# An expert's 176 inner rows as 112 and 64 in place of 88 and 88, and the 64 rows' two halves stacked in one operand

## The chip, the core and the metric

One Trainium2 chip, one of its cores. The engines are named as the profile names them: PE is TensorE (PEld its weight loads), DVE is VectorE, ACT is ScalarE, POOL is GpSimd, SP is the queue that starts most transfers. The metric is the device time of one execution, in microseconds (us).

## The reference

A transformer layer with adaptive layer norm, then a mixture of experts. The change touches the second part only: 2048 tokens of width 256, 16 experts of which each token takes 4, with an inner width of 176, and one shared expert with an inner width of 704.

```
g = jnp.einsum('nh,ehi->eni', h, w_gate)            # i = 176
u = jnp.einsum('nh,ehi->eni', h, w_up)
y = jnp.einsum('eni,eih->enh', jax.nn.silu(g) * u, w_down)
routed = jnp.einsum('enh,ne->nh', y, comb)          # comb: 4 experts a token
shared = jax.nn.silu(h @ sh_gate) * (h @ sh_up) @ sh_down   # 704 wide
return routed + sg * shared
```

## The kernel before

**How numbers are held.** Each matmul operand is kept as a high half (the value rounded to the matmul's format) and a low half (the rest). A product is three matmuls, in `PARTS`: high by high, high by low, low by high, given as (stationary, moving) pairs (0,0), (0,1), (1,0). ACT writes the high half with a copy out of PSUM, DVE the low half with a subtraction (`low_half`, L954, which also serves all other operands).

**The blocks.** Attention and the dense feed-forward take the first 665 us or so. Then the tokens are sorted by expert into 79 blocks of 128 rows. The weights of all experts lie in one tile, `wE`, and a block reads its expert's at an offset that PE loads into a register (`value_load`, L1864). For block i:

- PE turns the block's input (`turn_block`, L1855, two transposes); ACT (`high_hT`, L841) and DVE (`low_hT`) write its halves.
- PE computes gate and up together (`block_gate_up`, L1870): six matmuls of 352 columns. ACT takes silu (L847), DVE multiplies (L1372) into `hid_b`, 128 tokens by 176.
- PE turns `hid_b` (`turn_hidden`, L1881) as two transposes of 88 columns, into partitions 0 to 87 of one bank, beside each other. ACT (`high_hidT`, L853) and DVE (`low_hidT`) write the halves, one 88x256 instruction each.
- PE multiplies by the down weights (`block_down`, L1893): for each of the two groups of 88 rows the three `PARTS`, six matmuls of 256 columns that add up in one bank. ACT scales the result into `y_ring` (L861) and POOL scatters it (L628).

PE's order is written out by hand: in turn i it issues `turn_block(i+2)`, `block_gate_up(i+1)`, `turn_hidden(i)`, `block_down(i-1)`. So a block's down matmuls come one turn after its own transposes. All small tiles have two buffers.

**The shared expert.** 704 rows are five chunks of 128 and one of 64 (`SC_LAST`). For each of the four groups of 512 tokens and each chunk, `shared_gate_up` makes the hidden values and `shared_down` (L1831) multiplies by the down weights: 4 sub-blocks of 128 tokens by three matmuls of 256 columns, twelve a chunk, on 64 partitions for the last chunk. Two groups run before the blocks (calls 0 to 11), two after them (12 to 23). Call 11 stands just before the first `turn_block` of the loop.

Of the kernel before, what the change touches and what calls it, by code (L numbers as in the profile page):

```python
# [25 lines left out]
SC_FULL = I_SH // P  # L26
SC = SC_FULL + 1
SC_LAST = I_SH - SC_FULL * P
# [6 lines left out]
FRONT = FRONT_G * SC  # L35


HALF = I_MOE // 2
GU = 2 * I_MOE
EW = KD * GU + 2 * D  # L40

# [28 lines left out]
def adaln_moe_kernel(nc, x, condT, ada_w, bias, bqk, bv, wqkv, wo, w1, w2, router, shw_in, we_in, table, ident, out):  # L70
# [4 lines left out]
    ACT = mybir.ActivationFunctionType  # L75
# [20 lines left out]
    with ExitStack() as ctx:  # L96
# [20 lines left out]
        wE_flat = at("wE", 0, E * 2 * EW, f32r)  # L117
# [51 lines left out]
        id_sb = sb("id_sb", [P, P])  # L169
# [80 lines left out]
        h_blk, sil_b, hid_b = (blocks_own(m, n) for m, n in ((RING, HROW), (2, I_MOE), (2, I_MOE)))  # L250
# [22 lines left out]
            return (shw_b if late else shw)[:, first:first + w]  # L273

        def sh_down(late, c, s):
            rows = P if c < SC_FULL else SC_LAST
            first = 2 * SW * c + (s + 1) * sh_cols(c) - D
            return (shw_b if late else shw)[0:rows, first:first + D]

# [154 lines left out]
        def gated(i, rows):  # L434


            r = pair_of(i)
            return UP[r][:, :] if rows == P else GATE[r][0:rows, :]
# [4 lines left out]
        def pair_of(i):  # L443

            return (i + (i >= FRONT)) % 2
# [211 lines left out]
        def _(act):  # L657
# [191 lines left out]
            def high_hidT(i):  # L849
                act.wait_ge(s_hid_turned, i + 1)  # L850
                if i >= 2:
                    act.wait_ge(s_down_b, i - 1)
                nc.scalar.activation(hidT_b[0:HALF, i % 2, 0], HIDT_B[i % 2][0:HALF, 0:2 * P], ACT.Copy)\  # L853
                    .then_inc(s_hidT_high, 1)

            def keep_y(i):
# [57 lines left out]
        def _(dve):  # L914
# [38 lines left out]
            def low_half(target, whole, high):  # L953
                return nc.vector.tensor_tensor(target, whole, high.bitcast(f32), ALU.subtract)  # L954
# [355 lines left out]
            def shared_low(i):  # L1310
                rows = P if i % SC < SC_FULL else SC_LAST
                dve.wait_ge(s_hidden_high, i + 1)
                r = pair_of(i)
                hid = sh_hid[i >= FRONT]
                low_half(hid[0:rows, r, 1], gated(i, rows), hid[0:rows, r, 0]).then_inc(s_hidden_low, 1)

            def keep_shared(g):

# [54 lines left out]

            def low_hidT(i):
                dve.wait_ge(s_hidT_high, i + 1)
                low_half(hidT_b[0:HALF, i % 2, 1], HIDT_B[i % 2][0:HALF, 0:2 * P], hidT_b[0:HALF, i % 2, 0])\
                    .then_inc(s_hidT_low, 1)

            def destinations(n, own):

# [110 lines left out]
        def _(pe):  # L1491
# [327 lines left out]
            def shared_down(i):  # L1819
                g, c = divmod(i, SC)  # L1820
                rows = P if c < SC_FULL else SC_LAST
                pe.wait_ge(s_hidden_low, i + 1)
                if i == 0:
                    pe.wait_ge(s_h_kept, 2 * TG)
                elif i == FRONT:
                    pe.wait_ge(s_y_kept, BLOCKS)
                elif c == 0:
                    pe.wait_ge(s_sh_kept, BG * g)
                for b in range(BG):
                    for n, (s, m) in enumerate(PARTS):  # L1830
                        last = nc.tensor.matmul(DOWN[b // 2][:, D * (b % 2):D * (b % 2) + D],  # L1831
                                                sh_hid[i >= FRONT][0:rows, pair_of(i), s, T * b:T * b + T],
                                                sh_down(i >= FRONT, c, m),
                                                start=c == 0 and n == 0 and b % 2 == 0,
                                                stop=c == SC - 1 and n == len(PARTS) - 1, skip_group_check=True)
                last.then_inc(s_sh_down, 1)

            def blocks_to_all():
# [37 lines left out]
            def turn_hidden(i):  # L1876
                pe.wait_ge(s_hid, i + 1)
                if i >= 2:
                    pe.wait_ge(s_hidT_low, i - 1)
                for k in range(2):  # L1880
                    last = nc.tensor.transpose(HIDT_B[i % 2][0:HALF, P * k:P * k + P],  # L1881
                                               hid_b[i % 2][:, HALF * k:HALF * k + HALF], id_sb[:, :])
                last.then_inc(s_hid_turned, 1)

            def block_down(i, first):
                pe.wait_ge(s_hidT_low, i + 1)
                if i < 2:
                    pe.wait_ge(s_sh_kept, BG * FRONT_G)
                else:
                    pe.wait_ge(s_y_kept, i - 1)  # L1890
                for k in range(2):
                    for n, (s, m) in enumerate(PARTS):
                        last = nc.tensor.matmul(Y_B[i % 2][:, 0:D], hidT_b[0:HALF, i % 2, s, P * k:P * k + P],  # L1893
                                                wE_flat[0:HALF, bass.ds(first + (m * EW + KD * GU + D * k), D)],
                                                start=k == 0 and n == 0, stop=k == 1 and n == len(PARTS) - 1)
                last.then_inc(s_down_b, 1)

            for i in range(FRONT):
# [108 lines left out]
```

## Time and profile before

| | |
|---|---|
| median of 3 runs | 953.63 us (953.49 to 954.85) |
| profiled execution | 957.57 us, of which the span of the trace is 955.8 us |
| PE busy | 906.9 us (95%) |
| DVE, ACT, POOL busy | 571.2, 487.8, 271.9 us |
| block down matmuls (L1893) | 474, busy 75.7 us |
| shared down matmuls on 64 rows | 48 of 288 |

In the trace's rows a matmul (PE) is listed with the time from its start to its modelled end. Matmuls overlap, so the step from one start to the next is what one costs, not the length in its row. A weight load (PEld) belongs to each matmul and normally runs beside the matmul ahead of it. `88*128` in a row means 88 contraction rows by 128 stationary columns.

### The profile page before, as it was taken

To read this page: it belongs to the slowest core of one execution; us is meant where nothing else is said; L and a number is where in the kernel's file an instruction comes from. 1 tells how busy PE (TensorE), PEld (TensorE's weight loads), DVE (VectorE), ACT (ScalarE), POOL (GpSimd) and SP (SyncE) were. 2 spreads that over 40 slices of the span, in tenths; PEclk is the share of its full clock that TensorE was granted. 3 is DMA by queue.
4 is the path that set the end of the run, shared out by engine and by line. 5 is a ranking of instruction groups with operands and counts; after the bars stand their busy time and mean duration, and the time that the engine had idled before them with its cause. 6 is when DMAs were issued, how large, how long until landed. Compare 5 with 4: busy or idle time off the path is not lost.

```text
span 955.8 us, 17681 instructions
## 1 busy us (share of the span) xinstructions
PE 906.9 (95%) x5693; PEld 808.8 (85%) x5693; DVE 571.2 (60%) x1301; ACT 487.8 (51%) x1300; POOL 271.9 (28%) x220
## 2 busy tenths in 40 slices
PE   4899999999999999996999999999989899999996
PEld 4788989898989889895898877877878899999885
DVE  5844545545455464547547567775776655555786
ACT  2545454545455455443454555555546566666721
POOL 1330301103021020045000252377772344444300
PEclk9899999999999999998999999999999999999998
DMA  5999999200010010120000300334836334436472
GB/s 186 291 284 264 292 276 278 54 16 33 0 49 0 0 49 0 49 88 23 1 1 24 125 23 23 123 109 145 324 88 226 103 114 124 119 115 233 138 243 89
DMA packets 80562, 112.86 MB, mean 118 GB/s; under 512 B 6889, under 2 KB 69486, under 8 KB 80240
## 3 DMA queue, kind: packets, MB, share of 16 engines
q1 hardware_dynamic: 37712, 54.23, 18.0%
q10 hardware_dynamic: 35920, 40.60, 16.6%
q0 software_dynamic: 6864, 17.19, 5.0%
q8 instruction: 37, 0.61, 0.3%
q14 instruction: 29, 0.24, 0.1%
HBM read 54.35 MB, written 59.60 MB: 119 GB/s over the span
## 4 chain that ended last, share of the span: by engine, by line
PE 81%; DVE 12%; ACT 3%; issue 2%; DMA 1%; POOL 1%; SPq 0%; DVEq 0%; ACTq 0%; POOLq 0%
PE bank L1495 44%; PE bank L1870 8%; PE bank L1579 6%; PE bank L1893 6%; PE bank L1558 5%; PE bank L1567 3%; PE bank L1831 3%; PE bank L1881 2%; PE bank L1855 2%; DVE hid_area L954 1%; DVE negm L1016 1%; DVE acc L1475 1%; DVE wE L954 1%; DVE stats L939 1%; DMA bv_sb<-in_bv 1%
## 5 line engine op out<-in xcount | busy, mean ns | idle before, releaser
L954 DVE TENSOR_TENSOR hid_area<-bank,hid_area 128x512 fp32r<-128x512 f32 (+2 forms) x266 | 140.6, 530 | 169.1 <-ACT hid_area L704 112.9
L1495 PE MATMUL bank<-tok_area,arena_a 128*128 128x512 f32 x768 | 208.2, 407 | 5.4 <-DVE tok_area L954 4.8
L1495 PEld LDWEIGHTS bank<-tok_area,arena_a 128*128 128x128 f32 x768 | 139.4, 192 | 30.9 <-DVE tok_area L954 5.2
L689 ACT ACTIVATE work<-bank,negm 128x128 f32<-128x128 f32 x256 | 90.5, 367 | 98.8 <-DVE negm L1016 98.7
L682 ACT ACTIVATE work<-bank,bqk_sb 128x512 f32<-128x512 f32 x128 | 88.3, 690 | 72.3 <-PE bank L1495 72.2
L1495 PE MATMUL bank<-arena_a,tok_area 128*128 128x256 f32 x768 | 108.9, 292 | 0.0
L628 POOL DMA_INDIRECT ys<-y_ring,dest x79 | 77.2, 977 | 110.8 <-ACT y_ring L861 86.8
L423 POOL TENSOR_TENSOR arena_a<-raw,fixed 128x1536 fp32r<-128x1536 f32 x7 | 19.7, 2812 | 284.9 <-DMA bv_sb<-in_bv 284.9
L1870 PE MATMUL bank<-wE,hid_area 128*128 x474 | 96.1, 338 | 4.2 <-DVE hid_area L954 2.1
L1495 PEld LDWEIGHTS bank<-arena_a,tok_area 128*128 128x128 f32 x768 | 97.3, 193 | 0.0
L1495 PE MATMUL bank<-hid_area,x_area 128*128 128x512 f32 x384 | 96.1, 399 | 0.0
L1870 PEld LDWEIGHTS bank<-wE,hid_area 128*128 128x128 f32 x474 | 74.2, 188 | 9.2 <-issue 7.0
L1495 PEld LDWEIGHTS bank<-hid_area,x_area 128*128 128x128 f32 x384 | 69.8, 188 | 14.0 <-DVE hid_area L954 0.5
L1037 DVE TENSOR_TENSOR work<-bank,bv_sb 128x512 f32<-128x512 f32 x64 | 44.1, 691 | 61.0 <-PE bank L1495 57.8
L1893 PE MATMUL bank<-wE,hid_area 88*128 x474 | 75.7, 295 | 0.0
L1013 DVE TENSOR_REDUCE rmax<-bank 128x4 f32<-128x512 f32 x64 | 44.2, 691 | 44.1 <-PE bank L1558 44.1
L1579 PEld LDWEIGHTS bank<-work 128*128 128x128 f32 x512 | 65.2, 192 | 4.6 <-ACT work L697 1.8
L1579 PE MATMUL bank<-work 128*128 128x128 f32 x512 | 67.9, 275 | 1.1 <-DVE hid_area L954 1.1
L1558 PE MATMUL bank<-work 128*128 128x128 f32 x512 | 67.3, 274 | 0.0
L1558 PEld LDWEIGHTS bank<-work 128*128 128x128 f32 x512 | 64.7, 191 | 2.5
L1893 PEld LDWEIGHTS bank<-wE,hid_area 88*128 88x128 f32 x474 | 61.2, 190 | 0.4 <-issue 0.3
L704 ACT ACTIVATE hid_area<-bank 128x512 fp32r<-128x512 f32 x64 | 38.3, 598 | 44.5 <-PE bank L1579 44.4
(177 smaller groups left out, 1513.0 us busy)
## 6 DMA issues: line engine op xcount, KB each, us to landing
hs<-h_even ACTq DMA_DIRECT2D x1, 36448.0 KB, 153.5
work<-hs SPq DMA_DIRECT2D x79, 134.0 KB, 2.6
we_raw<-in_we SPq DMA_DIRECT2D x16, 608.0 KB, 6.6
y_all<-ys SPq DMA_DIRECT2D x8, 1024.0 KB, 10.5
raw<-in_wqkv SPq DMA_DIRECT2D x8, 768.0 KB, 5.0
work<-in_x SPq DMA_DIRECT2D x4, 512.0 KB, 6.5
raw<-in_wo SPq DMA_DIRECT2D x8, 256.0 KB, 4.9
raw<-in_w SPq DMA_DIRECT2D x2, 1024.0 KB, 5.8
```

Of the source, the lines that this page charges most:

```text
L628: pool.indirect_dma_start(out=ys, out_offset=bass.IndirectOffsetOnAxis(ap=dest[:, i:i + 1], axis=0), in_=y_blk[i % Y_RING], in_offset=None ...
L682: nc.scalar.activation(dst, PROJ[tile % 2][:, :], ACT.Identity, bias=bqk_sb[:, r, tile:tile + 1]).then_inc(s_qk_kept, 1)
L689: last = nc.scalar.activation(probs[:, m, i], SC_BANK[m][:, i * T:i * T + T], ACT.Exp, bias=negm[:, m, i:i + 1], scale=SCALE, accum_out=rs ...
L704: nc.scalar.activation(o_hl[:, 0, :, 256 * m:256 * m + 256], OB[:, :].rearrange("p (h n) -> p h n", h=HG), ACT.Copy).then_inc(s_o_high, 1)
L954: return nc.vector.tensor_tensor(target, whole, high.bitcast(f32), ALU.subtract)
L1013: nc.vector.tensor_reduce(rmax[:, m], SC_BANK[m][:, :].rearrange("p (i n) -> p i n", i=4), AX.X, ALU.max)\
L1037: nc.vector.tensor_tensor(v_sb[:, j % 2, 2 * tile:2 * tile + 2], PROJ[tile][:, :].rearrange("p (b n) -> p b n", b=2), bv_sb[:, r].unsqueez ...
L1495: last = nc.tensor.matmul(out_ap, stationary(s), moving(m), start=start and i == 0, stop=stop and i == len(PARTS) - 1)
L1558: last = nc.tensor.matmul(SC_BANK[m][:, i * T:i * T + T], qT[:, j % 2, h, col:col + T], kT[:, j % 2, h, col:col + T], start=True, stop=True)
L1579: last = nc.tensor.matmul(OB[:, col:col + T], v_sb[:, j % 2, 2 * m + b, h * DH:h * DH + DH], probsT[:, m, HG * b + h], start=True, stop=True)
L1870: last = nc.tensor.matmul(GU_B[i % 2][:, 0:GU], hT_b[:, i % 2, s, P * k:P * k + P], wE_flat[:, bass.ds(first + (m * EW + k * GU), GU)], st ...
L1893: last = nc.tensor.matmul(Y_B[i % 2][:, 0:D], hidT_b[0:HALF, i % 2, s, P * k:P * k + P], wE_flat[0:HALF, bass.ds(first + (m * EW + KD * GU ...
```

## The change

**Experts.** The 176 rows are cut as 112 and 64 (`MAIN`, `REST`). `turn_hidden` makes one transpose of 112 columns and one of 64. The halves of the 112 rows are written as before. The high half of the 64 rows goes to partitions 0 to 63 and their low half below it, to partitions 64 to 127 of the same columns. The down weights of the 64 rows are stored twice in DRAM's array, on partitions 0 to 63 and 64 to 127. One matmul on 128 partitions then gives high by high and low by high at once, and one on 64 partitions gives high by low: five down matmuls a block in place of six. ACT and DVE each issue two instructions of 128 columns in place of one of 256.

**Shared expert.** The last chunk's 64 rows are handled in the same manner: two matmuls for each sub-block (128 rows, then 64) in place of three, eight a chunk in place of twelve.

```diff
-HALF = I_MOE // 2
+REST = 64
+MAIN = I_MOE - REST
@@ sh_down
-            rows = P if c < SC_FULL else SC_LAST
+            rows = P if c < SC_FULL or s == 0 else SC_LAST
@@ high_hidT (ACT)
-                nc.scalar.activation(hidT_b[0:HALF, i % 2, 0], HIDT_B[i % 2][0:HALF, 0:2 * P], ACT.Copy)\
+                nc.scalar.activation(hidT_b[0:MAIN, i % 2, 0, 0:P], HIDT_B[i % 2][0:MAIN, 0:P], ACT.Copy)
+                nc.scalar.activation(hidT_b[0:REST, i % 2, 0, P:2 * P], HIDT_B[i % 2][0:REST, P:2 * P], ACT.Copy)\
                     .then_inc(s_hidT_high, 1)
@@ shared_low (DVE)
-                low_half(hid[0:rows, r, 1], gated(i, rows), hid[0:rows, r, 0]).then_inc(s_hidden_low, 1)
+                low = hid[0:rows, r, 1] if rows == P else hid[rows:2 * rows, r, 0]
+                low_half(low, gated(i, rows), hid[0:rows, r, 0]).then_inc(s_hidden_low, 1)
@@ low_hidT (DVE)
-                low_half(hidT_b[0:HALF, i % 2, 1], HIDT_B[i % 2][0:HALF, 0:2 * P], hidT_b[0:HALF, i % 2, 0])\
-                    .then_inc(s_hidT_low, 1)
+                low_half(hidT_b[0:MAIN, i % 2, 1, 0:P], HIDT_B[i % 2][0:MAIN, 0:P], hidT_b[0:MAIN, i % 2, 0, 0:P])
+                low_half(hidT_b[REST:2 * REST, i % 2, 0, P:2 * P], HIDT_B[i % 2][0:REST, P:2 * P],
+                         hidT_b[0:REST, i % 2, 0, P:2 * P]).then_inc(s_hidT_low, 1)
@@ shared_down (PE)
+                    parts = PARTS if rows == P else ((0, 0), (0, 1))
+                    for n, (s, m) in enumerate(parts):
+                        depth = P if m == 0 else rows
...
-                                                sh_hid[i >= FRONT][0:rows, pair_of(i), s, T * b:T * b + T],
+                                                hid[0:depth, pair_of(i), s, T * b:T * b + T],
@@ turn_hidden (PE)
-                for k in range(2):
-                    last = nc.tensor.transpose(HIDT_B[i % 2][0:HALF, P * k:P * k + P],
-                                               hid_b[i % 2][:, HALF * k:HALF * k + HALF], id_sb[:, :])
+                nc.tensor.transpose(HIDT_B[i % 2][0:MAIN, 0:P], hid_b[i % 2][:, 0:MAIN], id_sb[:, :])
+                nc.tensor.transpose(HIDT_B[i % 2][0:REST, P:2 * P], hid_b[i % 2][:, MAIN:I_MOE], id_sb[:, :])\
@@ block_down (PE)
-                for k in range(2):
-                    for n, (s, m) in enumerate(PARTS):
-                        last = nc.tensor.matmul(Y_B[i % 2][:, 0:D], hidT_b[0:HALF, i % 2, s, P * k:P * k + P],
-                                                wE_flat[0:HALF, bass.ds(first + (m * EW + KD * GU + D * k), D)],
-                                                start=k == 0 and n == 0, stop=k == 1 and n == len(PARTS) - 1)
+                for n, (s, m) in enumerate(PARTS):
+                    nc.tensor.matmul(Y_B[i % 2][:, 0:D], hidT_b[0:MAIN, i % 2, s, 0:P],
+                                     wE_flat[0:MAIN, bass.ds(first + (m * EW + KD * GU), D)], start=n == 0, stop=False)
+                for m, rows in ((0, 2 * REST), (1, REST)):
+                    last = nc.tensor.matmul(Y_B[i % 2][:, 0:D], hidT_b[0:rows, i % 2, 0, P:2 * P],
+                                            wE_flat[0:rows, bass.ds(first + (m * EW + KD * GU + D), D)],
+                                            start=False, stop=m == 1)
```

On PE, one turn of the block loop before, from the transposes of a block's hidden values to the next block's gate and up. A row is a line of the kernel, the output tile, the input tiles, the output's shape; ISA rows are register steps of the sequencer:

```order
L1881 MATMUL bank2<-id_sb_93,work2_86 88x128 [waits s_hidT_low,s_hid]
L1881 MATMUL bank2<-id_sb_93,work2_86 88x128
L1893 ISA [waits s_y_kept,s_hidT_low]
L1893 MATMUL bank7<-wE_58,hid_area_83 128x256
L1893 ISA
L1893 MATMUL bank7<-wE_58,hid_area_83 128x256 x2
L1893 ISA
L1893 MATMUL bank7<-wE_58,hid_area_83 128x256
L1893 ISA
L1893 MATMUL bank7<-wE_58,hid_area_83 128x256 x2
L1855 MATMUL bank5<-id_sb_93,work2_86 128x128 [waits s_hT_low,s_h_loaded_3]
```

The same turn after the change (L1888 and L1889 are the transposes, L1899 and L1903 the down matmuls):

```order
L1888 MATMUL bank2<-id_sb_93,work2_86 112x128 [waits s_hidT_low,s_hid]
L1889 MATMUL bank2<-id_sb_93,work2_86 64x128
L1899 ISA [waits s_y_kept,s_hidT_low]
L1899 MATMUL bank7<-wE_58,hid_area_83 128x256
L1899 ISA
L1899 MATMUL bank7<-wE_58,hid_area_83 128x256 x2
L1903 ISA
L1903 MATMUL bank7<-wE_58,hid_area_83 128x256
L1903 ISA
L1903 MATMUL bank7<-wE_58,hid_area_83 128x256
L1863 MATMUL bank5<-id_sb_93,work2_86 128x128 [waits s_hT_low,s_h_loaded_3]
```

One down matmul is gone; the register steps, the waits and the order stay. The last L1903 matmul, on 64 contraction rows, stands between one on 128 rows and the next block's transposes.

On DVE, in the part of the block loop where it also writes experts' low halves, before and after:

```order
L954 TENSOR_TENSOR hid_area<-bank,hid_area 128x256 [waits s_hT_high]
L1372 TENSOR_TENSOR work_86<-bank,work_86 128x176 [waits s_hid_turned,s_silu_b]
L954 TENSOR_TENSOR hid_area<-bank,hid_area 88x256 [waits s_hidT_high]
L954 TENSOR_TENSOR wE<-we_raw_69,wE 128x608 [waits s_we_high]
L954 TENSOR_TENSOR hid_area<-bank,hid_area 128x256 [waits s_hT_high]
```

```order
L957 TENSOR_TENSOR hid_area<-bank,hid_area 128x256 [waits s_hT_high]
L1376 TENSOR_TENSOR work_86<-bank,work_86 128x176 [waits s_hid_turned,s_silu_b]
L957 TENSOR_TENSOR hid_area<-bank,hid_area 112x128 [waits s_hidT_high]
L957 TENSOR_TENSOR hid_area<-bank,hid_area 64x128
L957 TENSOR_TENSOR wE<-we_raw_69,wE 128x608 [waits s_we_high]
```

The 88x256 instruction has become two; ACT's 88x256 copy has done the same.

## Rows read from the trace of the kernel before

**Rows 1.** The page's first part: busy us, share, instructions of each engine.
```profile
PE 906.9 (95%) x5693; PEld 808.8 (85%) x5693; DVE 571.2 (60%) x1301; ACT 487.8 (51%) x1300; POOL 271.9 (28%) x220
```

**Rows 2.** Stretches: length, then busy us (instructions) of PE, PEld, DVE, ACT, POOL; clock; DMA.
```profile
726.02:759.16 33.14, 29.67 (x211) 27.37 (x210) 23.71 (x67) 21.86 (x58) 12.97 (x13) 1.00 0.48 152
759.16:896.53 137.37, 137.22 (x1009) 131.83 (x1008) 83.13 (x272) 87.89 (x257) 60.40 (x63) 1.00 0.43 131
```

**Rows 3.** Waits, 740 to 880 us: us in total, times, longest.
```profile
PE bank L1870 <- DVE hid_area L954: 1.5, 1, 1.5
```

**Rows 4.** Chain that ended last: start us, us, what. Blocks' down matmuls are L1893.
```profile
726.02 0.72 PE bank L1893 x6
...
751.88 0.36 DVE hid_area L954
752.24 0.71 DVE wE L954
...
759.16 0.72 PE bank L1893 x6
...
785.17 0.71 PE bank L1893 x6
785.89 0.22 PE bank L1855 x2
786.11 0.99 PE bank L1870 x6
...
787.32 0.71 PE bank L1893 x6
...
896.53 0.71 PE bank L1893 x6
...
949.33 2.08 PE bank L1831 x12
```

**Rows 5.** PE's sequencer (PEldq) in one turn: duration ns min/median/max, first and last start.
```profile
L1864 PEldq TENSOR_LOAD <-block_we x1: 308/308/308, 802.5 to 802.5; - x1
L1870 PEldq FUSED_REGOPS  x4: 42/46/46, 803.3 to 803.7; - x4
```

**Rows 6.** PE and PEld in order of time: start, us, line, operands, count [idle before].
```profile
695.15 1.48 PEld L1831 LDWEIGHTS bank<-shw,hid_area 64*128 64x128 f32 x12 [0.35 <-issue]
...
719.41 0.32 PE L1870 MATMUL bank<-wE,hid_area 128*128 x1
719.66 0.38 PE L1831 MATMUL bank<-shw,hid_area 64*128 64x256 f32 x1
719.88 0.52 PE L1831 MATMUL bank<-shw,hid_area 64*128 64x256 f32 x3
...
721.08 0.28 PE L1831 MATMUL bank<-shw,hid_area 64*128 64x256 f32 x1
721.29 0.33 PE L1855 MATMUL bank<-id_sb,work 128*128 128x128 f32 x1
...
721.73 0.48 PE L1870 MATMUL bank<-wE,hid_area 128*128 x2
...
800.89 0.28 PE L1893 MATMUL bank<-wE,hid_area 88*128 x1
...
801.42 0.64 PE L1870 MATMUL bank<-wE,hid_area 128*128 x3
...
803.04 0.25 PEld L1855 LDWEIGHTS bank<-id_sb,work 128*128 128x128 f32 x2
803.39 0.94 PEld L1870 LDWEIGHTS bank<-wE,hid_area 128*128 128x128 f32 x6
```

**Rows 7.** Groups by line and shape: count, busy us, mean ns of one, idle before.
```profile
L853 ACT ACTIVATE hid_area<-bank 88x256 fp32r<-88x256 f32 x79 | 30.0, 380 | 0.8 <-PE bank L1881 0.8
L847 ACT ACTIVATE work<-bank 128x176 f32<-128x176 f32 x79 | 25.0, 317 | 38.8 <-PE bank L1870 38.8
L954 DVE TENSOR_TENSOR hid_area<-bank,hid_area 88x256 fp32r<-88x256 f32 x79 | 33.1, 419 | 0.5 <-ACT hid_area L853 0.5
L1372 DVE TENSOR_TENSOR work<-bank,work 128x176 f32<-128x176 f32 x79 | 26.9, 340 | 25.5 <-ACT work L847 25.0
```

More of the change, by code:

```diff
@@ L1828, in shared_down @@
                     pe.wait_ge(s_sh_kept, BG * g)
+                hid = sh_hid[i >= FRONT]
                 for b in range(BG):
-                    for n, (s, m) in enumerate(PARTS):
+                    parts = PARTS if rows == P else ((0, 0), (0, 1))
+                    for n, (s, m) in enumerate(parts):
+                        depth = P if m == 0 else rows
                         last = nc.tensor.matmul(DOWN[b // 2][:, D * (b % 2):D * (b % 2) + D],
-                                                sh_hid[i >= FRONT][0:rows, pair_of(i), s, T * b:T * b + T],
+                                                hid[0:depth, pair_of(i), s, T * b:T * b + T],
                                                 sh_down(i >= FRONT, c, m),
                                                 start=c == 0 and n == 0 and b % 2 == 0,
-                                                stop=c == SC - 1 and n == len(PARTS) - 1, skip_group_check=True)
+                                                stop=c == SC - 1 and n == len(parts) - 1, skip_group_check=True)
                 last.then_inc(s_sh_down, 1)
@@ L1879, in turn_hidden @@
                     pe.wait_ge(s_hidT_low, i - 1)
-                for k in range(2):
-                    last = nc.tensor.transpose(HIDT_B[i % 2][0:HALF, P * k:P * k + P],
-                                               hid_b[i % 2][:, HALF * k:HALF * k + HALF], id_sb[:, :])
-                last.then_inc(s_hid_turned, 1)
+                nc.tensor.transpose(HIDT_B[i % 2][0:MAIN, 0:P], hid_b[i % 2][:, 0:MAIN], id_sb[:, :])
+                nc.tensor.transpose(HIDT_B[i % 2][0:REST, P:2 * P], hid_b[i % 2][:, MAIN:I_MOE], id_sb[:, :])\
+                    .then_inc(s_hid_turned, 1)
             def block_down(i, first):
@@ L1890, in block_down @@
                     pe.wait_ge(s_y_kept, i - 1)
-                for k in range(2):
-                    for n, (s, m) in enumerate(PARTS):
-                        last = nc.tensor.matmul(Y_B[i % 2][:, 0:D], hidT_b[0:HALF, i % 2, s, P * k:P * k + P],
-                                                wE_flat[0:HALF, bass.ds(first + (m * EW + KD * GU + D * k), D)],
-                                                start=k == 0 and n == 0, stop=k == 1 and n == len(PARTS) - 1)
+                for n, (s, m) in enumerate(PARTS):
[5 more added lines that the diff above has]
+                                            start=False, stop=m == 1)
                 last.then_inc(s_down_b, 1)
@@ L1958 @@
         dn[0:many] = sh_dn[rows]
+        if many < P:
+            dn[many:2 * many] = sh_dn[rows]
         chunks += [both, dn]
@@ L1964 @@
     dn = np.zeros((E, P, 2, D), np.float32)
-    dn[:, 0:HALF] = w_down.reshape(E, 2, HALF, D).transpose(0, 2, 1, 3)
+    dn[:, 0:MAIN, 0] = w_down[:, 0:MAIN]
+    dn[:, 0:REST, 1] = dn[:, REST:2 * REST, 1] = w_down[:, MAIN:I_MOE]
     experts = np.concatenate([both, dn.reshape(E, P, 2 * D)], 2)
```

## The prediction

> **What bounds the kernel now.** I read the engines' busy shares first: PE is busy for 95% of the span [rows 1], and the change touches only the blocks and the shared expert, so I went to the stretches. From the first block's down matmuls at 726.02 us to the end of the steady part at 896.53 there are two regimes [rows 2, 4]. Blocks 0 to 13 take 33.14 us, 2.55 us a block; PE has gaps there (29.67 us busy), since DVE also writes experts' low halves. One such place: the low half of the hidden values at 751.88, then 0.71 us for an expert's, and PE waits for that [rows 4]. Blocks 13 to 76 take 137.37 us for 63 blocks, 2.18 us a block, and PE is busy for 137.22 of them, at the full granted clock (1.00, so 2.4 GHz). DVE and ACT are at 61% and 64% there. The list of waits from 740 to 880 us has a single wait of PE for DVE's hidden values, 1.5 us [rows 3]. So PE's own work sets the pace, and a block's price is read from the chain: 0.71 us for six down matmuls (0.119 each), 0.22 for two transposes of the input, 0.97 to 0.99 for gate and up, another 0.22 for the hidden values' transposes [rows 4]; the latter is what lies between the end of gate and up at 787.10 and 787.32. That sums to 2.12, which many blocks show; the mean is 0.06 more. In the rows of the chain the extra sits before gate and up. PE's sequencer explains it: it begins the register load at 802.5, and issues the first gate-and-up step at 803.3; the last transposes' weight loads start at 803.04 and are over at 803.29, and the next weight load starts only at 803.39, 0.10 us idle [rows 5, 6]. So the sequencer runs hardly ahead of PE, and the 0.06 is its doing.
>
> **What the change removes.** One down matmul of 256 columns a block: 0.119 us (0.71 / 6) [rows 4]. The sequencer loses one load and one matmul to issue; its four register steps for down stay, as the order shows. If nothing else cost anything, PE's own floor would be 2.12 - 0.12 = 2.00 us a block. The sequencer's cycle of about 2.18 would shrink by something between nothing and that one matmul's time; 0.06, the middle, is used in rival A alone.
>
> **What it adds on PE: matmuls on 64 rows among others on 128.** The kernel before has these in the shared expert's last chunk, four times, and there the trace shows what the change between row counts costs. Going in: the last gate-and-up matmul starts at 719.41, and its kind takes 0.16 a piece (0.97 / 6). The first 64-row matmul starts at 719.66, 0.09 late. Its weight load wasn't ahead of it: it starts with it. So the second starts 0.22 later, not 0.12, another 0.10. Going in costs 0.19 [rows 6]. The other site shows the weight loads idle for 0.35 us until the first 64-row one, by no releaser but "issue" [rows 6]. Going out, into the same transposes that follow in the block loop: from the last 64-row matmul (721.08) to the second gate-and-up matmul (721.73) there are 0.65 us; between the same two in a steady block (800.89 to 801.42) there are 0.53. Out costs 0.12 [rows 6]. Together 0.31 us for one excursion. The trace has no excursion of a single matmul, but the two prices sit at its two ends, and neither end depends on the eleven between. Bounds: 0.18 if the two gaps of 0.09 stay and the loads are hidden after all, 0.38 if the way out costs as much as the way in. I take 0.31, the sum that was read at the very neighbours that the block will have.
>
> A block then needs 2.12 - 0.12 + 0.31 = 2.31 us of PE, against 2.18 now. The sequencer needs 2.18 or less for a block, so it gains a lead again and its 0.06 of stalls goes. Over 63 blocks: +0.13 x 63 = **+8.2 us** (with 0.18: 2.18, no change; with 0.38: +12.6).
>
> The Trainium skill has a rule that speaks against this change (TensorEngine Tiling (Array Packing), Key Properties): a change of tiling mode drains TensorE. By that rule each crossing between 128 and 64 rows empties the array, and the trace agrees as to the fact (0.09 us late, and the load not ahead), while the page gives no price; the sum doesn't use it.
>
> Whether the 112-row operands cost anything: 88-row matmuls stand among 128-row ones now without a gap (0.119 each), so nothing. The 64-column transpose has no row of its own; the nearest is the 88-column one, which fits into 0.22 for two. I take nothing. The upper end is an excursion of its own (0.31 a block), a rival below.
>
> **ACT and DVE.** Each issues two of 128 columns for one of 88x256. From 176 columns (317 ns on ACT, 340 on DVE) and 256 (380 and 419) [rows 7] the slope is about 0.8 and 1.0 ns a column, so 128 columns are 0.28 and 0.29 us: +0.18 and +0.16 a block, as bounds from above, since neighbours may overlap. In the steady part both have 0.8 us a block to spare, and the down matmuls come a turn after the transposes, so nothing (cover: PE's own 2.31 us). In blocks 0 to 13 it counts where DVE's chain is what PE waits for: about 3 places at some 0.3, 0.9 us; the other 10 blocks pay PE's +0.15. Together **+2.4 us** (ends 0.5, when the waits swallow it, and 4).
>
> **Shared expert, last chunk.** Twelve matmuls with one way in and out become eight that alternate 128, 64, 128, 64: eight crossings of 0.19, since 128-row matmuls wait for their load as well. 8 x 0.119 + 8 x 0.19 = 2.47 us against 12 x 0.119 + 2 x 0.19 = 1.81: +0.66, four times **+2.6 us**. The last one is on the chain too (2.08 us at 949.33, followed by nothing but the final sums) [rows 4]. Ends -1.9 (four matmuls less, no crossing paid) and +3.5. The last blocks and their tail: +0.3.
>
> **The sum.** 8.2 + 2.4 + 2.6 + 0.3 = +13.5 us. The profiled execution took 957.57 us, 1.8 more than its span, and 3.9 more than the median of the runs; the sum changes it to 971.1, and I put the same difference on the median: 953.6 + 13.5 = 967.1, so 967.
>
> **Rivals.**
> *A, faster.* The crossing is cheap when one matmul alone is concerned, because its load can be taken ahead. The point from which it decides: an excursion under 0.18 us (0.12 for the matmul, 0.06 for the sequencer's stall). At no cost at all the block goes to what the sequencer allows, 2.12: 79 x -0.06 = -4.7, and the shared chunks -1.9: 947 us. For it: no single 64-row matmul is in the trace. Against it: both sites of the trace show the load not ahead. 0.10.
> *B, no change.* The load of the lone 64-row matmul hides, the two gaps stay: 0.18 an excursion. Blocks 0, shared chunks 8 x 0.21 in place of 1.81, nearly 0, early blocks +0.5 to 1: 954.5. The Trainium skill would point here (TensorE: Matmul & The Clock Gate, the list of what overlaps in packed matmuls): weight loads run beside matmuls in flight where the row groups differ, and by that rule the load into 64 rows might be early. The rows at 719.66 and 695.15 say otherwise. 0.07.
> *C, twice as dear.* The 64-column transpose pays a crossing each way as well: +0.31 a block, 79 x 0.31 = 24.5 more, 992 us. For it: 64 columns are half of the array as 64 rows are. Against: nothing in the trace, for it has no such transpose. 0.08.
> *D, DVE becomes the bound* in blocks 0 to 13: it is busy for 23.71 of 33.14 us there, +0.16 a block makes 26, still below. It only adds to the early term: 970. 0.05, inside the range.
>
> **Chances and range.** The forecast 0.70, with A, B, C and D as given. The range takes in B at the low end, 954; at the high end it has 0.38 for an excursion, +12.6, with the upper ends +4 and +3.5 and the tail's 0.3, 974, and some more if the steady part keeps the sequencer's 0.06 a block (3.8), 978. That leaves out A and C, 18 in 100. 0.2% is 1.9 us, about what a measurement of this kernel can tell from no change: faster 0.10, same 0.07, slower 0.83.
>
> **What the profile after would show.** L1903's matmul on 64 rows starts about 0.2 us after the one ahead of it, the next transpose 0.3 after that, and the block's period is 2.31 us with less than 0.05 of scatter, because the sequencer no longer stalls. The 64-column transpose is followed by the down matmuls without a gap (else C). Weight loads have idle time before 64*128 put down to "issue". The last chunk's eight matmuls take some 2.4 us. Wrong if the period is under 2.18: then the crossing is cheap for one matmul (A), or the gaps are there but the loads hidden (B).

## The result and the profile after

The changed kernel took **972.94 us** (970.41 to 973.6, 4 runs), the one before 953.56 (953.01 to 954.85, 4 runs beside them). The ratio is 1.0196, 95% interval 1.0175 to 1.0218: 19.4 us slower, where the forecast was 967 with a range from 954 to 978. The sign, the range and the mechanism held. The size is 6 us above the sum.

First part of the page of the kernel after, to lay beside [rows 1] (busy us, share of the span, instructions):

```profile
span 971.8 us, 17649 instructions
...
PE 926.7 (95%) x5598; PEld 808.3 (83%) x5598; DVE 587.1 (60%) x1380; ACT 492.8 (51%) x1379; POOL 274.3 (28%) x220
```

PE has 95 matmuls less (79 in the blocks, 16 in the shared expert) and is busy for 20 us longer. DVE has 79 instructions more and 16 us more work.

The chain of the kernel after, two blocks of the steady part (start us, us, what). L1899 and L1903 are the down matmuls on 112 rows and on 128 and 64 rows, L1863 the transposes of the input, L1878 gate and up, L1888 and L1889 the hidden values' transposes:

```profile
809.66 0.43 PE bank L1903 x2
810.09 0.37 PE bank L1863 x2
810.45 0.97 PE bank L1878 x6
811.42 0.11 PE bank L1888
811.53 0.11 PE bank L1889
811.64 0.36 PE bank L1899 x3
812.00 0.43 PE bank L1903 x2
```

One turn is 2.34 us from L1903 to L1903. Against [rows 4], the two transposes of the input have gone from 0.22 to 0.37. The pair of L1903 takes 0.43, where two down matmuls before took 0.24 (0.71 / 3). That is the excursion: 0.19 at its beginning, 0.15 at its end. The 64-column transpose takes 0.11 like its neighbour.

The same place instruction by instruction, PE and then its weight loads (start us, us, line, operands, count):

```profile
811.84 0.59 PE L1903 MATMUL bank<-wE,hid_area 128*128 x2
812.36 0.44 PE L1863 MATMUL bank<-id_sb,work 128*128 128x128 f32 x2
...
811.37 0.42 PEld L1899 LDWEIGHTS bank<-wE,hid_area 112*128 112x128 f32 x3
811.72 0.50 PEld L1903 LDWEIGHTS bank<-wE,hid_area 128*128 128x128 f32 x2
812.36 0.20 PEld L1863 LDWEIGHTS bank<-id_sb,work 128*128 128x128 f32 x2
812.52 0.79 PEld L1878 LDWEIGHTS bank<-wE,hid_area 128*128 128x128 f32 x5
```

The load for the transposes starts at 812.36, in the moment in which the transposes themselves start: it was not ahead. The next one, for L1878, is again (812.52, its matmul 812.55).

To find where the 19.4 us are, I cut both traces at the starts of the same down matmuls: the first of the shared expert's (674.66 us before, 671.30 after), and those of blocks 0, 13, 15 and 76.

| stretch | before | after | difference | of which clock |
|---|---|---|---|---|
| shared expert to block 0 | 51.12 | 55.09 | +3.97 | about 2.5 |
| blocks 0 to 13 | 33.14 | 34.64 | +1.50 | |
| blocks 13 to 15 | 4.25 | 5.90 | +1.65 | about 1.3 |
| blocks 15 to 76 (61) | 133.12 | 142.63 | +9.51 | |
| block 76 to the end | 59.51 | 62.24 | +2.73 | about 0.6 |

They sum to 19.36 where the medians differ by 19.38. Each trace is one execution, so that they meet so closely is luck. (The spans differ by 16.0 only, because the profiled execution of before came 3.4 us later to the first of these points, through code that both share.)

The fourth row is the forecast's term. Most of the third (all but the 0.3 that two more blocks cost at the rate of the fourth) and more than half of the first were in no term. They are TensorE's clock. Stretches of the kernel after (length, busy us and instructions of PE, PEld, DVE, ACT, POOL, then granted clock, DMA share, GB/s):

```profile
707.00:712.40 5.40, 5.38 (x13) 4.24 (x14) 2.50 (x3) 2.93 (x5) 5.07 (x2) 0.50 0.32 84
759.00:763.30 4.30, 3.75 (x16) 3.20 (x17) 1.61 (x8) 1.22 (x4) 0.78 (x1) 0.67 0.08 27
964.00:967.50 3.50, 3.37 (x8) 1.88 (x8) 0.05 (x1) 0.00 (x0) 0.00 (x0) 0.67 0.00 0
```

and the answering stretches of before:

```profile
709.60:712.60 3.00, 2.91 (x13) 2.47 (x14) 2.33 (x3) 1.89 (x4) 2.60 (x1) 1.00 0.46 112
...
949.00:951.50 2.50, 2.06 (x12) 1.77 (x12) 0.35 (x2) 0.00 (x0) 0.00 (x0) 0.78 0.01 3
```

The same twelve matmuls of 512 columns, in the shared expert, in the chain of after (the next matmul starts 5.26 us behind the first of them, before 2.80):

```profile
699.08 5.83 DVE wE L957
...
706.88 0.14 issue
707.02 5.46 PE bank L1500 x12
```

and in the chain of before:

```profile
709.69 2.97 PE bank L1495 x12
```

In both kernels PE had been idle for 3.31 us ahead of them, for a low half on DVE that comes behind 5.83 us of an expert's low half. After it they ran at 0.50 (1.2 GHz), before at 1.00 (2.4 GHz). Whether that belongs to the change is asked of the experiments below.

### The profile page after: what moved, and what is told of

Read it like the earlier page. It is cut to its first block, busy times and chain, and to the rows that moved or that the text cites. A ratio compares the mean times of both kernels' runs of the same rounds, so it can differ in the third digit from the quotient of the medians.

```text
span 971.8 us, 17649 instructions
## 1 busy us (share of the span) xinstructions
PE 926.7 (95%) x5598; PEld 808.3 (83%) x5598; DVE 587.1 (60%) x1380; ACT 492.8 (51%) x1379; POOL 274.3 (28%) x220
## 4 chain that ended last, share of the span: by engine, by line
PE 82%; DVE 11%; ACT 2%; issue 2%; DMA 1%; POOL 1%; SPq 0%; DVEq 0%; ACTq 0%; POOLq 0%
PE bank L1500 44%; PE bank L1878 8%; PE bank L1584 6%; PE bank L1563 5%; PE bank L1903 3%; PE bank L1839 3%; PE bank L1572 3%; PE bank L1899 3%; PE bank L1863 3%; DVE hid_area L957 1%; DVE acc L1480 1%; DVE wE L957 1%; PE bank L1888 1%; PE bank L1889 1%; DMA bv_sb<-in_bv 1%
## 5 line engine op out<-in xcount | busy, mean ns | idle before, releaser
L957 DVE TENSOR_TENSOR hid_area<-bank,hid_area 112x128 fp32r<-112x128 f32 (+3 forms) x345 | 153.0, 444 | 161.5 <-ACT hid_area L706 111.0
L1878 PE MATMUL bank<-wE,hid_area 128*128 x474 | 96.4, 338 | 3.9 <-DVE hid_area L957 2.2
L1878 PEld LDWEIGHTS bank<-wE,hid_area 128*128 128x128 f32 x474 | 75.1, 190 | 4.7 <-issue 4.5
L1026 DVE TENSOR_TENSOR work<-work,rinv 128x512 f32<-128x512 f32 x64 | 60.4, 944 | 2.2
L699 ACT ACTIVATE work<-bank 128x512 f32<-128x512 f32 x64 | 38.2, 597 | 42.8 <-PE bank L1572 42.7
```

The source lines that it names most:

```text
L1026: nc.vector.tensor_tensor(probs[:, m], probs[:, m], rinv[:, m].unsqueeze(2).to_broadcast([P, 4, T]), ALU.mult).then_inc(s_probs, 1)
L1878: last = nc.tensor.matmul(GU_B[i % 2][:, 0:GU], hT_b[:, i % 2, s, P * k:P * k + P], wE_flat[:, bass.ds(first + (m * EW + k * GU), GU)], st ...
```

## The experiments

The theory is the forecast's: the lone matmul on 64 rows costs about 0.3 us, at its two ends, and outweighs the matmul that is saved. The rivals that were left: the time comes from elsewhere (the 64-column transpose, the two instructions more on DVE and ACT, the shared expert), or the fifth matmul would have saved nothing anyway. All times are medians; each ratio is against runs of the kernel before on the same chip in the same series, whose medians were 955.04, 954.44 and 954.54 us.

### The 64-row matmuls on 128 rows

The stacked operand makes this easy: below the 64 rows of high weights stand the same weights again, and below the high hidden values their low halves. (The sum gains the low half times the low weights, a term that the exact product has as well.) Everything else of the change stays.

```diff
-            rows = P if c < SC_FULL or s == 0 else SC_LAST
+            rows = P
...
-                for m, rows in ((0, 2 * REST), (1, REST)):
+                for m, rows in ((0, 2 * REST), (1, 2 * REST)):
...
-                        depth = P if m == 0 else rows
+                        depth = P
```

> The changed kernel, but the matmul on 64 contraction rows is made on 128 (and in the shared expert's last chunk too). The lower 64 rows then add the product of the low halves, a term of the order of the rounding that both kernels leave out; nothing is left out. Theory 1 (crossing between 128 and 64 rows costs PE 0.33 us a block): the crossings are gone, a block takes what the larger of PE's floor (2.13 - 0.12 = 2.01) and the sequencer's cycle (about 2.12) allows, so 2.01 to 2.12; the shared chunk's eight matmuls take 0.95 us. Time 953.6 - 4.7 (or up to 13) - 1.9: 940 to 948 us. Rival 2 (the four more instructions of ACT and DVE a block, or the 64-column transpose, are the cost): block stays at 2.3, time above 965 us.

It took 955.61 us (952.38 to 961.48, 10 runs), ratio 1.0009 (0.9992 to 1.0027): the loss is gone, and no gain has come, where 940 to 948 was expected. Blocks 15 to 76 take 2.171 us each, against 2.338 after and 2.182 before. So the crossing between row counts was the loss; the 64-column transpose and the two extra instructions on DVE and ACT, all still there, were not. The chain of this kernel:

```profile
811.39 0.22 PE bank L1863 x2
811.61 1.11 PE bank L1878 x6
...
813.54 0.22 PE bank L1863 x2
813.76 1.07 PE bank L1878 x6
```

The transposes are back at 0.22. But gate and up take 1.11 and 1.07, not 0.97. Groups of weight loads by shape from 765 to 885 us show why (count, busy us, mean ns, idle before), here of this kernel:

```profile
L1878 PEld LDWEIGHTS bank<-wE,hid_area 128*128 128x128 f32 x330 | 51.6, 187 | 7.9 <-issue 4.2
```

of the kernel before:

```profile
L1870 PEld LDWEIGHTS bank<-wE,hid_area 128*128 128x128 f32 x332 | 51.9, 187 | 2.6 <-issue 0.7
```

and of the kernel after:

```profile
L1878 PEld LDWEIGHTS bank<-wE,hid_area 128*128 128x128 f32 x306 | 48.3, 189 | 0.0
...
L1863 PEld LDWEIGHTS bank<-id_sb,work 128*128 128x128 f32 x103 | 10.4, 140 | 6.7
L1903 PEld LDWEIGHTS bank<-wE,hid_area 128*128 128x128 f32 x52 | 9.9, 190 | 0.0
L1903 PEld LDWEIGHTS bank<-wE,hid_area 64*128 64x128 f32 x52 | 9.5, 183 | 7.0
```

In these 55 blocks the load of gate and up waits for 7.9 us where PE's own work has become shorter, 0.14 a block, at the register load that picks the expert. Before it was 2.6, 0.05 a block. After it is 0.0, and the idle time stands at the two ends of the 64-row matmul instead: 7.0 and 6.7 us in 51 blocks, 0.14 and 0.13 each. A fifth matmul saved gives 0.12 to PE, and PE's sequencer takes it back.

### The blocks' part alone

The shared expert is as before; the blocks are as after.

```diff
-            rows = P if c < SC_FULL or s == 0 else SC_LAST
+            rows = P if c < SC_FULL else SC_LAST
...
-                    parts = PARTS if rows == P else ((0, 0), (0, 1))
+                    parts = PARTS
...
```

> The experts' part of the change alone; the shared expert's last chunk has its twelve matmuls as before. Theory 1: block period 2.34 as in the changed kernel, each last chunk 1.6 us again in place of 2.4, so 4 x 0.8 = 3.2 us less than the changed kernel, with the last one's 1.3 in place of 0.8: 969 us (967 to 970). Rival: the shared chunks were free, 972 to 973 us. The two stretches at half clock may stay or go; if they stay, this kernel is 2 to 4 us above the sum of the block's periods.

967.96 us (967.12 to 970.11, 4 runs), ratio 1.0146 (1.0127 to 1.0166). The period is 2.339, as after. The rest, 5.0 us by the medians, goes with the shared part. In the stage table this run has 51.18 us from the shared expert to block 0, as before (51.12, and 55.09 after), and 60.71 from block 76 to the end (62.24 after). Not all of that is the last chunks' matmuls: about 2.5 us is the twelve matmuls, which ran at full clock here. This execution had its half clock elsewhere: the mean granted clock is 0.66 from 750 to 760 us, and blocks 0 to 15 take 40.8 us (40.5 after, 37.4 before).

```profile
705.05 2.99 PE L1500 MATMUL bank<-tok_area,shw 128*128 128x512 f32 x12 [3.31 <-DVE hid_area L957]
```

### The crossing alone, in the kernel before

Nothing of the change is in; only the block's sixth down matmul takes 64 of its 88 rows. The kernel leaves out the other 24 rows of that low-by-high product.

```diff
+                        deep = 64 if (k, n) == (1, 2) else HALF
-                        last = nc.tensor.matmul(Y_B[i % 2][:, 0:D], hidT_b[0:HALF, i % 2, s, P * k:P * k + P],
+                        last = nc.tensor.matmul(Y_B[i % 2][:, 0:D], hidT_b[0:deep, i % 2, s, P * k:P * k + P],
```

> The kernel before, in which the sixth down matmul of a block uses 64 of its 88 contraction rows (24 rows of one low-by-high product are left out). Nothing is removed, moved or added. Theory 1: the crossing alone, 0.31 to 0.34 us a block less the 0.05 of stalls that it hides: block 2.44 to 2.47, +21 to +23 us, 975 to 977 us. Rival 2 (ACT, DVE, transposes or the sequencer): no change, 953.6 us. Rival 3 (a lone crossing is only dear next to an operand of stacked halves): below 960.

975.89 us (4 runs), ratio 1.0221 (1.0204 to 1.0238). One smaller operand, the same count of instructions, and the kernel is 20.9 us slower; the period is 2.450. Its chain:

```profile
813.22 0.90 PE bank L1894 x6
814.12 0.37 PE bank L1855 x2
814.49 0.97 PE bank L1870 x6
```

Down matmuls 0.90 in place of 0.71, transposes 0.37 in place of 0.22: the same 0.19 and 0.15 as in the changed kernel. This is the price by itself. It also has a half-clock stretch in the shared expert, whose code is that of before, behind the same idle time:

```profile
706.53 4.51 PE L1495 MATMUL bank<-tok_area,shw 128*128 128x512 f32 x12 [3.31 <-DVE hid_area L954]
```

### Two crossings a block

As above, with the third and the sixth down matmul on 64 rows, so two products of a block lack 24 rows each. The third has 88-row matmuls on both sides.

```diff
-                        deep = 64 if (k, n) == (1, 2) else HALF
+                        deep = 64 if (k, n) in ((0, 2), (1, 2)) else HALF
```

> The kernel before with two lone 64-row matmuls a block, the third and the sixth of the down matmuls (24 rows of each low-by-high product are left out). e3_crossing_only had one at a period of 2.454 us against PE's floor of 2.12. Theory: the second pays as well, and with a 128-column load on its way out it costs 0.38: period 2.83, 953.6 + 79 x 0.65 = 1005 us. Rival (a fixed price a block, the drain happens once): 2.45, 976 us.

1005.85 us (1 run). The period is 2.843, so the second crossing adds 0.39. The six down matmuls in its chain:

```profile
812.56 1.29 PE bank L1894 x6
813.85 0.37 PE bank L1855 x2
```

1.29 is 0.39 above the 0.90 of the kernel before this one; with 0.19 for a way in, the way out into an 88-row matmul costs 0.20, against 0.15 into the transposes. That is the 0.38 that the forecast had as its upper bound, true here and not at the place of the change.

### Before, without the register load

To separate PE's own work from its sequencer: the expert's offset is fixed in the code, so there is no register load and no register step. What the kernel leaves out is the choice of the expert; matmuls and waits are the same.

```diff
-                first = pe.value_load(block_we[0:1, i:i + 1], min_val=0, max_val=(E - 1) * 2 * EW)
+                first = min(i, E - 1) * 2 * EW
```

> The kernel before with a fixed offset of the weights for each block in place of the one loaded into a register (block i takes expert min(i, 15)): the choice of the expert is left out, the work and every wait are the same. It tests the reason for the 0.05 us by which a block lies over PE's floor. If PE's sequencer is late because of the register load and the eight register steps: period 2.13 without scatter, 65 x 0.05 = 3 us less, 950 us. If the scatter has another cause (memory traffic, the queue of ACT or DVE): 953.6 us.

949.58 us (949.48 to 949.7, 4 runs), ratio 0.9947 (0.993 to 0.9963). The period falls from 2.182 to 2.118. The weight loads of gate and up, 765 to 885 us:

```profile
L1870 PEld LDWEIGHTS bank<-wE,hid_area 128*128 128x128 f32 x339 | 53.2, 188 | 0.2 <-DVE hid_area L954 0.2
```

So the 0.06 a block of the kernel before is the sequencer's (the whole gains 5.5 us, of which the steady blocks are 3.9; blocks 0 to 13 take 31.16 us in place of 33.14), and PE's floor for six down matmuls is 2.12. Against that floor the crossing costs 2.450 - 2.118 = 0.33 us. The shared expert, unchanged again, has the half clock as well: its twelve matmuls take 4.44 us behind 3.31 of idle time.

```profile
706.29 4.44 PE L1495 MATMUL bank<-tok_area,shw 128*128 128x512 f32 x12 [3.31 <-DVE hid_area L954]
```

### Five matmuls on 128 rows, without the register load

> e1_all128 (five down matmuls, all on 112 or 128 rows) with fixed weight offsets in place of the register load and the eight register steps (block i takes expert min(i, 15): the choice of the expert is left out). Theory: in e1_all128 PE waits for its sequencer, whose cycle is 2.12 to 2.17 us a block, so the matmul that is gone bought nothing. Without the register work PE's own floor shows: 2.12 - 0.12 = 2.00 us a block, 61 x 0.17 = 10 us less than e1_all128 in the steady part: 943 to 946 us. Rival (PE's floor didn't fall with the fifth matmul, because the 64-column transpose or the two instructions of ACT and DVE hold it): period stays over 2.10, 949 us or more.

The edit joins those of the first and the fifth experiment, and the kernel leaves out the choice of the expert again. 943.33 us (941.24 to 945.16, 4 runs), ratio 0.9875 (0.986 to 0.9889), period 2.015. PE's floor with five down matmuls is 0.10 below that with six, and 0.323 below the changed kernel. In its chain the excursion's two pieces, 0.43 and 0.37 after, are whole again:

```profile
810.48 0.24 PE bank L1903 x2
810.73 0.22 PE bank L1863 x2
```

### Five matmuls on 128 rows, with four waits less

The first experiment's kernel, keeping its register load, but without four waits a block of PE that other waits make superfluous.

```diff
-                if i >= 2:
-                    pe.wait_ge(s_hT_low, i - 1)
...
-                if i >= 2:
-                    pe.wait_ge(s_hid, i - 1)
...
-                if i >= 2:
-                    pe.wait_ge(s_hidT_low, i - 1)
...
-                else:
-                    pe.wait_ge(s_y_kept, i - 1)
```

> e1_all128 without four of PE's waits a block that another wait already implies: for block i's input transposes the wait for low halves that gate and up of block i-2 waited for; for gate and up the wait that the hidden values' transposes had; for these, the one that down had; for down, the wait for ACT's copy of two blocks before, which ACT made ahead of a copy that is waited for. Nothing is left out of the computation. If the sequencer bounds the block (cycle 2.17 at e1), each wait less takes 0.03 to 0.05 us off its cycle: period 2.00 to 2.05, 7 to 10 us less than e1_all128: 945 to 948 us. If PE waits for something else: 955 us as e1_all128.

948.26 us (942.89 to 950.87, 6 runs), ratio 0.9923 (0.9904 to 0.9943): **faster than both kernels**, by 0.8% against before. The period is 2.025, 0.146 below that of the first experiment (2.171) and 0.01 above the floor. The loads of gate and up are hardly kept waiting any more:

```profile
L1874 PEld LDWEIGHTS bank<-wE,hid_area 128*128 128x128 f32 x356 | 56.0, 188 | 0.8 <-issue 0.5
```

By the program's order none of the four can hold PE: PE has waited for a later count of the same signal, or for work that comes behind it, before it gets there. What they cost was the sequencer's time, at least 0.037 us apiece (0.146 / 4; the period has come down nearly to PE's floor, so more may be hidden). The steady part alone gives 61 x 0.157 = 9.6 us against before, though the whole gains 6. In the trace, which is of the slowest of the six runs, the rest went in two places. Blocks 0 to 13 take 34.72 us here and 13 to 15 take 5.85, before 33.14 and 4.25. The shared expert to block 0 takes 53.66, before 51.12; its twelve matmuls take 5.46, at half clock. From 757 to 763.5 us this kernel has the clock at 0.50:

```profile
757.00:763.50 6.50, 5.21 (x21) 4.70 (x20) 3.17 (x12) 2.37 (x7) 0.97 (x1) 0.50 0.05 18
```

### The shared expert's last chunk in another order

After, but in the last chunk first the four matmuls on 128 rows and then the four on 64, two crossings in place of eight.

```diff
-                for b in range(BG):
-                    parts = PARTS if rows == P else ((0, 0), (0, 1))
-                    for n, (s, m) in enumerate(parts):
+                parts = PARTS if rows == P else ((0, 0), (0, 1))
+                turns = [(b, n) for b in range(BG) for n in range(3)] if rows == P else [(b, n) for n in range(2) for b in range(BG)]
+                for b, n in turns:
```

> The changed kernel with the last chunk's eight matmuls in another order: first the four on 128 rows, then the four on 64, so two crossings in place of eight. Theory (a crossing costs, the number of 64-row matmuls doesn't): 8 x 0.12 + 0.38 = 1.33 us a chunk in place of 2.4, 4 x 1.05 = 4 us less: 968 to 969.5 us. Rival (each 64-row matmul is slow in itself): no change, 973 us.

969.12 us (966.76 to 974.02, 4 runs), ratio 1.0169 (1.0148 to 1.0191), 3.8 below after by the medians and 2.6 by the ratios, whose intervals overlap. The traces tell the two apart. The eight matmuls in this kernel, start and duration:

```profile
689.49 1.29 PE L1840 MATMUL bank<-shw,hid_area 128*128 128x256 f32 x8
```

and in the kernel after:

```profile
691.71 2.46 PE L1839 MATMUL bank<-shw,hid_area 128*128 128x256 f32 x8
```

Six crossings less are 1.17 us, 0.195 each. Three of the six are ways in and three are ways out, so this is their mean.

### The shared part alone on 128 rows, and with four waits less

The kernel before, with the last chunk stacked, all its matmuls on 128 rows (eight in place of twelve); then the same with the four waits taken out of the blocks as above.

```diff
+                    parts = PARTS if rows == P else ((0, 0), (0, 1))
-                    for n, (s, m) in enumerate(PARTS):
+                    for n, (s, m) in enumerate(parts):
+                        depth = P
...
```

> The kernel before with only the shared expert's last chunk changed: the two halves stacked, eight matmuls a chunk, all on 128 rows, so no crossing where there were two. Nothing is left out. By the prices read so far: 4 x (4 x 0.12 + 2 x 0.19) = 3.4 us less where PE sets the pace: 951 us. If the last two chunks hide behind DVE's sums: 1.7 us less, 952.7.

> e14_shared128_only with the four implied waits a block taken off PE as well; the experts keep 88 and 88 rows and six down matmuls. Expected: the period falls from 2.18 to PE's floor, 2.12, 65 x 0.06 = 4 us less than e14: 947 us. Against e12_all128_fewer_waits (948.3 with a period of 2.025) it tells what ACT's and DVE's extra instructions cost in blocks 0 to 15: in the steady part e12 gains 6 us over this one; if e12 isn't faster, they give it back there.

The first: 954.01 us (952.49 to 956.74, 12 runs), ratio 0.9992 (0.998 to 1.0004). Four times four matmuls and two crossings less would be 3.4 us; 0.5 arrives, not told apart from nothing. Its trace shows what the first chunk's saving meets: PE waits for DVE's hidden values for 4.56 us in place of 3.31, and then does its twelve matmuls at half clock. (The first line is DVE's and the second POOL's, ahead of that wait.)

```profile
698.15 7.09 DVE L954 TENSOR_TENSOR wE<-we_raw,wE 128x1216 fp32r<-128x1216 f32 x1
698.38 5.57 POOL L623 TENSOR_TENSOR wE<-we_raw,wE 128x1216 fp32r<-128x1216 f32 x2
...
707.36 5.46 PE L1496 MATMUL bank<-tok_area,shw 128*128 128x512 f32 x12 [4.56 <-DVE hid_area L954]
...
948.48 2.07 PE L1835 MATMUL bank<-shw_b,hid_b 128*128 128x256 f32 x8 [2.18 <-DVE hid_b L954]
```

The wait is long because of the first line: an expert's low half that takes DVE 1.4 us elsewhere takes 7.09 here, and 5.83 before. In all twelve traces it ends 1.29 us after POOL's two instructions on the same tile. So it looks as if POOL sets the end of this wait, and as if what PE saves ahead of it can't arrive; no run tests that.

The last chunk's eight at the end take 2.07 us, no less than the twelve of [rows 4], since the clock is falling there too.

The second: 951.08 us (949.65 to 957.65, 12 runs), ratio 0.9964 (0.9951 to 0.9977), period 2.121. The period is what was expected; the time is 4 us above the 947 expected, since the kernel without this edit lies as much above its own forecast. So the four waits are worth 2.9 us with six down matmuls and 7.3 with five (955.61 - 948.26; by the two ratios 8.2). With six, PE's floor of 2.12 is met soon; with five there is room down to 2.02. Of the best version's gain of 6.2 us, about half (3.5) comes without the stacked operand in the blocks.

## Why the prediction was right, and where it was short

**What bounds the kernel: right.** PE's own work and, 0.06 a block, its sequencer. The run without the register load took 0.064 off the period (2.182 to 2.118), and the chain shows the loads of gate and up without idle time.

**The price of the excursion: right, a little low.** 0.31 was taken, 0.32 to 0.34 is what the chain and two pairs of runs give (2.338 - 2.015 and 2.450 - 2.118). The way in was 0.19 as read from [rows 6]. The way out was 0.15, not 0.12. The steady term was +0.13 a block; it measured 2.338 - 2.182 = 0.156, so 9.5 us for 61 blocks where the forecast's rate gives 7.9. Reading an excursion of one matmul from the two ends of one of twelve worked.

The rule of the Trainium skill (TensorEngine Tiling (Array Packing), Key Properties) that a change of the tiling mode drains TensorE agrees with every crossing between 64 rows and more here, at 0.15 to 0.20 us each way. Between 88 and 128, or 112 and 128 rows, no run shows such a gap. The page gives no price.

**The sequencer gains a lead: right.** The loads of L1878 have 0.0 us of idle time after, 2.6 before, and turn follows turn with 2.34 to 2.35 us in the chain.

**The 64-column transpose and the 112-row operands cost nothing: right.** 0.11 and 0.11 in the chain, three L1899 matmuls in 0.36. Rival C falls, and with a period above 2.18 rival B too.

**ACT and DVE: not borne out.** 0.9 of the 2.4 us forecast for blocks 0 to 13 were DVE's and ACT's. These blocks cost 1.50 us more. The crossing alone, with ACT's and DVE's instructions as before, costs 1.65 there (34.79 against 33.14), and without the register load they take 31.20 us with the two pairs and 31.16 without. So the crossing is enough for what was measured, and no run shows the pairs' share; each figure is one trace. In the steady part DVE's pair is covered. Groups of the kernel after, by shape:

```profile
L957 DVE TENSOR_TENSOR hid_area<-bank,hid_area 112x128 fp32r<-112x128 f32 x52 | 15.2, 292 | 0.1
L957 DVE TENSOR_TENSOR hid_area<-bank,hid_area 64x128 fp32r<-64x128 f32 x51 | 14.5, 284 | 0.7
L855 ACT ACTIVATE hid_area<-bank 112x128 fp32r<-112x128 f32 x52 | 14.4, 277 | 0.0
L856 ACT ACTIVATE hid_area<-bank 64x128 fp32r<-64x128 f32 x52 | 13.4, 258 | 0.0
```

292 and 284 ns on DVE, 277 and 258 on ACT: the 0.29 and 0.28 of the slope. Rival D did not come up.

**The shared expert's last chunk: right, except where the clock falls.** 0.66 each was forecast for an alternation 128, 64, 128, 64. For the first chunk, from the start of the fourth matmul ahead of it to the start of the third behind it, before takes 3.18 us (694.16 to 697.34) and after 3.86 (690.80 to 694.66): +0.68. Two of the other three give the same. The first experiment, without a crossing, takes 2.33, so eight crossings are 1.53 us, 0.19 each. At the end of the kernel the eight take 3.37 against 2.06 for the twelve of before, +1.3, since the clock falls during them (0.67 against 0.78). Together 3.4 in place of 2.6.

**The clock: the step that is missing.** The sum took every duration as it stood in the trace of before, at the clock of before. About 2.5 us in the shared expert, 1.3 at block 13 and 0.6 in the last chunk are matmuls at half clock. At all three sites PE has just waited for DVE. The idle time was in the profile, and with it the risk; I had no term for it on either side.

Whether the change set it off is only partly answered. At the twelve matmuls it can't be said: two kernels whose code there is that of before, the crossing alone and the fixed offset, lost 1.5 us there, behind the same 3.31 us of idle time, while before and the blocks' part alone lost none. Of all twelve kernels these two are the only ones without a loss at that place. But each run has its mean granted clock: 0.986 to 0.988 in the four of after, 0.988 to 0.994 in the 46 of before in the experiments' series. Among 22 of these on one chip the six at 0.989 took 955.07 to 957.0 us and the four at 0.994 took 951.65 to 954.01, some 3 us less. The medians of after and before lie about as far apart in clock (0.9865 against 0.991 to 0.993). So, as an estimate, some 3 of the 19.4 us are a lower clock that the version after has in its usual run, and not only in its trace.

| term | forecast | measured |
|---|---|---|
| blocks 13 to 76 | +8.2 | +11.2, of which about 1.3 clock |
| blocks 0 to 13 | +2.4 | +1.5 |
| shared expert's last chunks | +2.6 | +3.4, of which 0.6 clock |
| tail besides | +0.3 | +0.7 |
| shared expert besides | none | +2.6, of which 2.5 clock |
| sum | +13.5 | +19.4 |

**Rival A was wrong in its own price.** It said that without a crossing the sequencer would let the block go down to 2.12, and the kernel to 947. With the crossing really gone, in the first experiment, the block stays at 2.171 and the kernel at 955.61. I had taken the sequencer's cycle to shrink with the matmul that is gone by half of its time; it shrank by hardly a tenth of it (2.182 to 2.171). What shortens it is what it steps through, the waits and register steps.

**What stays open.** Why the same idle time ahead of the same twelve matmuls ends in a full clock in one execution and in half in another. Each kernel's trace is one execution, so what the clock cost the best version in its usual run was not measured apart. Its mean granted clock is 0.984 to 0.988 in five of its six runs, at 947.54 to 950.87 us, and 0.992 in the sixth, at 942.89 us. Why DVE's instruction ahead of the long wait ends when POOL's do is open too.

## What to carry to other kernels

Among operands on more than 64 rows, don't put one matmul on 64: fill it up to 128 rows with something harmless, even if that does more work, or put all the 64-row ones in a row. Before a matmul is saved on a PE that is busy for all of a stretch, look at the idle time of its weight loads put down to "issue": there the sequencer is the next bound, and waits that never hold anything are worth more than the matmul. Where PE waits for several microseconds, price what follows at half clock as well as at full.

## What was not expected of the hardware

- The way into 64 rows costs 0.19 us, the way out 0.15 into transposes and 0.20 into matmuls, at 256 columns. It is paid by a lone matmul as by twelve, and a second excursion in a block adds as much again (0.33, then 0.39).
- A wait of PE whose condition has long been met costs at least 0.037 us of the sequencer's time: four fewer a block of 15 matmuls took its period from 2.171 to 2.025 us. The register load takes 0.30 us in the trace, and yet with the four waits gone, leaving it out as well gives only 0.01 more.
- A gap of 3.31 us on PE was followed by twelve matmuls in 2.97, 2.99, 4.44, 4.51 or 5.46 us in five kernels in which these twelve are the same. (With two crossings a block it was 3.29 and 4.58.) In the other six kernels, whose last chunk ahead of it is shorter, the gap was 4.55 to 4.57 and the twelve took 4.53 to 5.46, never at full clock throughout. The Trainium skill (TensorE: Matmul & The Clock Gate, the part on the clock gate) says that when the gate acts can differ from run to run of one kernel. What the runs show fits with that: the mean granted clock of the best version's six runs goes from 0.984 to 0.992. No kernel here was traced twice.
